# A selective scan on four engines: VectorE takes one of ScalarE's fourteen scaled copies of each round

## The reference, cut to what matters

```python
def selective_scan(u, delta, A, Bm, Cm, D):
    def step(h, inp):
        u_l, d_l, B_l, C_l = inp
        dA = jnp.exp(d_l[:, :, None] * A)
        h = h * dA + (d_l * u_l)[:, :, None] * B_l[:, None, :]
        y = jnp.einsum('bdn,bn->bd', h, C_l)
        return (h, y)
    ...
    return jnp.transpose(ys, (1, 0, 2)) + u * D
```

## Time and profile before

| | |
|---|---|
| median of 3 runs | 18361.85 us (18345.74 to 18377.84) |
| profiled execution | 18362.69 us, span 18360.9 us, mean granted clock 0.962 |
| busy share of the span | PE 88%, DVE 87%, ACT 79%, POOL 61% |
| first scan stage (`l0sf_`) | scans from 870.4 to 2913.8 us in the span |
| second scan stage (`l0sb_`) | the same work, about 3440 to 5485 us |
| granted TensorE clock in both | 1.00 |

### The profile page before, as it was taken

How to read it: one execution, slowest core, us unless ns; L and a number is a source line. 1 busy time by engine, 2 the same in 40 slices (tenths; PEclk the granted TensorE clock), 3 DMA queues, 4 the chain that set the end, 5 groups by cost and what they waited for, 6 DMA issues and landing times. The chain is left out here.

```text
span 18360.9 us, 268147 instructions
## 1 busy us (share of the span) xinstructions
PE 16077.0 (88%) x94216; PEld 11444.0 (62%) x94216; DVE 15910.4 (87%) x12063; ACT 14529.2 (79%) x23238; POOL 11254.5 (61%) x6343
## 2 busy tenths in 40 slices
PE   8799998899996788879888888888888888889798
PEld 3355554455552365455688888888888888647374
DVE  4799998799996486479899999999999999879698
ACT  7699996799992555557899999999999999745556
POOL 0099993499990475035688888888888888500201
PEclk9899999899997899989999999999999999999899
DMA  5788886788879677767777777777777777741323
GB/s 178 231 243 250 246 252 208 233 249 247 251 223 245 213 226 217 265 230 278 224 191 200 194 192 191 194 193 192 191 190 197 197 191 191 194 122 55 104 57 101
DMA packets 1043305, 3693.66 MB, mean 201 GB/s; under 512 B 162006, under 2 KB 196410, under 8 KB 1017404
## 3 DMA queue, kind: packets, MB, share of 16 engines
q1 hardware_dynamic: 815420, 3003.46, 53.8%
q0 software_dynamic: 147456, 536.94, 14.9%
q10 hardware_dynamic: 79104, 136.10, 2.4%
HBM read 2342.15 MB, written 796.94 MB: 171 GB/s over the span
## 5 line engine op out<-in xcount | busy, mean ns | idle before, releaser
L1832 DVE TENSOR_TENSOR_SCAN l1s_h<-l1s_da,l1s_pd 128x1024 f32<-128x1024 f32 x3072 | 6709.3, 2262 | 152.0 <-DMA l1s_h<-l1s_h 85.4
L1853 ACT ACTIVATE l1s_da<-l1s_dl,l1s_a 128x1024 f32<-128x1024 f32 x3072 | 3505.0, 1141 | 312.7 <-DVE l1s_h L1832 308.5
L1718 PE MATMUL l1s_pd<-l1s_bd,l1s_dut 128*128 128x128 f32 x18432 | 2847.5, 291 | 853.7 <-DVE l1s_h L1832 828.6
L1718 PEld LDWEIGHTS l1s_pd<-l1s_bd,l1s_dut 128*128 128x128 f32 x18432 | 2297.3, 191 | 1229.0 <-DVE l1s_h L1832 1092.0
L1870 ACT ACTIVATE l1s_dm<-l1s_dut,l1s_bt 128x384 f32<-128x384 f32 x5120 | 2888.2, 602 | 200.9 <-PE l1s_pd L1723 200.5
L1687 POOL TENSOR_TENSOR l1s_pb<-l1s_h,l1s_cc 128x1024 f32<-128x1024 f32 x1024 | 2423.4, 2367 | 843.7 <-DVE l1s_h L1832 802.6
L1687 POOL TENSOR_TENSOR l1s_pa<-l1s_h,l1s_cc 128x1024 f32<-128x1024 f32 x1024 | 2428.0, 2371 | 84.1 <-DMA l1s_h<-l1s_h 84.1
L1723 PE MATMUL l1s_pd<-l1s_id,l1s_dm 128*128 128x128 f32 x15360 | 2186.6, 273 | 0.1
L2702 POOL TENSOR_TENSOR l0sf_pr<-l0sf_h,l0sf_cc 128x1024 f32<-128x1024 f32 x768 | 1810.9, 2375 | 32.2 <-DVE l0sf_h L2784 27.0
L2702 POOL TENSOR_TENSOR l0sb_pr<-l0sb_h,l0sb_cc 128x1024 f32<-128x1024 f32 x768 | 1809.1, 2371 | 30.8 <-DVE l0sb_h L2784 26.8
L1723 PEld LDWEIGHTS l1s_pd<-l1s_id,l1s_dm 128*128 128x128 f32 x15360 | 1789.4, 142 | 0.6 <-ACT l1s_dm L1870 0.5
(11 more groups left out here) (323 smaller groups left out, 31362.7 us busy)
## 6 DMA issues: line engine op xcount, KB each, us to landing
l1s_cc<-crows SPq DMA_DIRECT2D x1024, 512.0 KB, 4.5
l1s_h<-l1s_h POOLq DMA_DIRECT2D x1024, 512.0 KB, 6.9
l0sf_cc<-l0crowsf SPq DMA_DIRECT2D x512, 512.0 KB, 6.3
l0sb_cc<-l0crowsb SPq DMA_DIRECT2D x512, 512.0 KB, 5.7
l0sf_cc<-l0crowsf SPq DMA_DIRECT2D x512, 256.0 KB, 8.5
l0sb_cc<-l0crowsb SPq DMA_DIRECT2D x512, 256.0 KB, 7.6
dls<-l1p_dl SPq DMA_DIRECT2D x192, 512.0 KB, 7.0
duts<-l1p_dut SPq DMA_DIRECT2D x64, 1536.0 KB, 6.6
```

The source lines that it names most:

```text
L1718: pe.matmul(pd[:, s % 2, blk * 128:blk * 128 + 128], dut[:, half, blk, j * 128:j * 128 + 128], bd[:, n, blk - SCALED, :], start=True, stop ...
L1832: dve.tensor_tensor_scan(tile(rnd, j), da[:, j, :], pd[:, s % 2, :], 0.0, ALU.mult, ALU.add)\
L1853: act.activation(da[:, j, :], dl[:, half, j, :], ACT.Exp, scale=a[:, HT * half + j, n:n + 1])\
```

## The change

VectorE makes the product of the seventh time block (index 6) for the second sequence (q = 1), in one `tensor_scalar` of 128x192 with the per-partition number B; ScalarE makes thirteen instead of fourteen. A new semaphore `multdve` tells TensorE, which now waits for four semaphores ahead of `turn_hi`.

```diff
@@ PE
                 def turn_hi(c, s):
                     pe.wait_ge(multhi, nth(c * ROUNDS + s // T))
                     pe.wait_ge(multlast, nth(c * ROUNDS + s // T))
+                    pe.wait_ge(multdve, nth(c * ROUNDS + s // T))
                     pe.wait_ge(scanhi, nth(c * STEPS + s - 1))
                     turn(s, 1).then_inc(trhi, 1)
@@ DVE
+                def multiply(c, rnd):
+                    if rnd % N == 0:
+                        loaded(dve, c, rnd // N)
+                    dve.wait_ge(trhi, nth(c * STEPS + (rnd - 1) * T - 1))
+                    out, src, b = scaled(c, rnd, LAST - 1, 1)
+                    dve.tensor_scalar(out, src, b, None, ALU.mult).then_inc(multdve, 1)
@@
                         scan_lo(c, s)
                         if not (first and s == 0):
                             scan_hi(c if s else c - 1, (s - 1) % STEPS)
+                        if j == 1 and not (final and rnd + 1 == ROUNDS):
+                            multiply(c + (rnd + 1) // ROUNDS, (rnd + 1) % ROUNDS)
                         at = s % (N * T) - 2
@@
+                multiply(0, 0)
                 chunks(dve, body)
@@ ACT
-                        for q in range(2):
+                        for q in range(1 if blk == LAST - 1 else 2):
                             out, src, b = scaled(c, rnd, blk, q)
                             ins = act.activation(out, src, ACT.Identity, scale=b)
```

More of the change, by code:

```diff
@@ L2609, in l0_scans @@
         s_u, s_y = r.dma_sem("u"), r.dma_sem("y")
-        aexp, anegd, cleared, multlo, multhi, multlast, expd, trlo, trhi, scanlo, scanhi, kept, prod, ysum, fin, passed = r.step_sems(
-            "aexp", "aneg", "cleared", "multlo", "multhi", "multlast", "expd", "trlo", "trhi", "scanlo", "scanhi", "kept", "prod", "ysum",
+        aexp, anegd, cleared, multlo, multhi, multlast, multdve, expd, trlo, trhi, scanlo, scanhi, kept, prod, ysum, fin, passed = r.step_sems(
+            "aexp", "aneg", "cleared", "multlo", "multhi", "multlast", "multdve", "expd", "trlo", "trhi", "scanlo", "scanhi", "kept", "prod", "ysum",
             "fin", "passed")
```

## The result

| | before | after |
|---|---|---|
| median | 18349.33 us (16 runs) | 18404.16 us (18395.22 to 18429.82, 16 runs) |
| ratio, 95% interval | | 1.0029, 1.0021 to 1.0037 |
| span of the profiled execution | 18360.9 us | 18400.3 us |

The account below looks back on a forecast made before the run. ACT bounds, with DVE and PE 0.6 us behind; after the change POOL does. 3 x 7.785 + 11 x 8.00 + 18.01 + 0.5 + 0.4 = 130.3 a half-chunk, +2.7, times 32 +86: 18448 us, range 18345 to 18560.

Parts of the forecast that it names:

- The bounds: Scan stages: ACT is the bound at 127.60 us a half-chunk, DVE and PE need 127.0, so at most 0.6 to gain.
- The exclusion on SBUF: DVE's new product and POOL's instructions wait for each other's whole instruction; POOL's round goes from 7.887 to 8.00 us.
- the named signs: Profile after: ACT busy 177 us less, product 0.5 to 0.8 ending 0.1 behind POOL's, POOL 8.0 a round, 130 between finishes.
- b: POOL's loss per round from waiting for DVE's new product: 0.11 us, at most 0.29.
- The room of PE: Between a low scan's end and the transposes needing it: a DVE wait of up to 0.3 us stays hidden.
- L: Time from the end of a round's first high scan to POOL's product of that step; to settle at about 0.5 us.
- `finish`: The two rounds per half-chunk holding finish, where DVE has no room: 18.01 us plus 0.5 for the two products.
- The rows of C: Rounds where POOL waits for a row of C, which a bounding POOL can't win back: 0.4 us a half-chunk.
- b = 0: Lower end: DVE's work fits into POOL's change of instruction; half-chunk 128.1 to 128.5, +16 to +29 us.
- the main case: POOL, delayed by DVE's product, sets the scan stages' pace: 130.3 us a half-chunk, +86 us; chance 0.58.
- The starved case: Rival: DVE can't get in between back-to-back POOL instructions and waits until POOL runs dry; 19060 to 19860 us, chance 0.17.

Follow-up runs that it names:

- experiment 1: Kernel before the change, with the seventh block's second-sequence product made by nobody, ScalarE making thirteen, no fourth wait; 18344.29 us, ratio 0.9995.
- experiments 2 to 4: Against the changed kernel: ScalarE makes all fourteen, VectorE's product goes to a spare tile, 1.0029; then a 128x64 transpose instead, 1.0006; last is experiment 4.
- experiment 4: Changed kernel without POOL's product of the eighth time block, which nobody makes, nor its semaphore; 18348.27 us, ratio 0.9994.
- experiments 6 and 8: Changed kernel, VectorE making the product only for rounds 3, 4, 5 of each half-chunk, 1.0009; the same with its input wait before the half-chunk's first scan, 1.0002.

## Why the prediction was right, and where its sizes were off

- **The bounds.** ACT at 127.6, the DVE and PE side at 127.0: shown by experiment 1. That nearly nothing could be gained was the step from which the rest followed.
- **The exclusion on SBUF, and who pays.** Shown by experiments 2 to 4 together: the loss stays without ScalarE's relief, and goes with either another kind of instruction or a POOL that isn't behind. The rule of the Trainium skill, "SBUF — State Buffer", section "Who interferes with whom", names `tensor_scalar` among the instructions that can enter a two-port mode and so contend with GpSimd; this case's trace agrees (0.83 beside POOL's product, 0.29 without one). Of the named signs these came: the product ending 0.1 behind POOL's, ACT's products 180 us less (177 forecast; the engine's whole busy time, of which the forecast spoke, fell by 124) and ACT waiting for DVE, POOL with almost no idle time outside `finish`. The length is at the upper end, 0.82 in the median where 0.5 to 0.8 was named, and POOL's 7.92 and the 129.0 between `finish`es are below the 8.0 and 130.
- **b was mis-sized: 0.11 forecast, 0.035 measured.** I scaled from an instruction that ended 0.28 behind POOL's. Here it ends 0.11 behind, and POOL's step across its change of instruction grows by only 0.033 (0.145 to 0.178). Nine rounds at 7.92 with five at 7.79 are 110.3, where 3 at 7.785 and 11 at 8.00 were 111.4: 1.1 too much.
- **The room of PE was mis-sized: 0.3 forecast, about 0.4 measured.** At a product of 0.60 the pitch is still 7.78 to 7.79, so a wait of 0.3 is hidden whole; at 0.83 the wait is 0.54 and costs 0.13 a round. That is why five rounds, not three, run at the old pace. It is one part of why L climbs to 0.76 instead of 0.5. The others are a slip in the forecast (a wait of L - 0.1, less 0.3 of room, costs 0.2 at L = 0.6, not 0.5) and the offset: the wait of 0.54 is L less 0.22, not less 0.1.
- **`finish` was mis-sized: +0.5 forecast, +0.75 measured.** Experiment 4 gives 0.23 of it to the second of the two rounds. The other 0.5 lies in the first one, which is entered with L settled: its product takes 0.83 where DVE has no room. From low scan to low scan, in a half-chunk of the second stage:

  | | first round with `finish` | second | rounds behind it |
  |---|---|---|---|
  | before | 9.74 | 8.26 | 7.78 |
  | experiment 4 | 9.74 | 8.50 | 7.78 |
  | the change | 10.26 | 8.50 | 7.78, then 7.92 |

- **The rows of C.** I added 0.4. The undisturbed half-chunk is 129.0 and the mean of twelve in the second stage 129.31, so it was 0.3, against 0 before in the same stage.
- Sum by the measured terms: 18.76 + 38.97 + 71.29 + 0.3 = 129.3, where 130.3 was forecast. The difference of 1.0 a half-chunk is the 31 us or so.
- **The lower end was summed too low.** For b = 0 the forecast has 128.1 to 128.5. With its own 0.5 for `finish` and 0.4 for the rows of C, 3 x 7.785 + 11 x 7.887 + 18.51 is 128.6 to 129.0, which is +33 to +46 us. So the measured +55 lies close to its case of b = 0, not halfway between that and the main case as its figures have it.
- **The starved case (0.17)** did not come in the change. Its mechanism exists, as experiments 6 and 8 show, but only one product at a time: a missed turn did not bring on the next.

## What to carry to other kernels

Work moved from an engine that is 99% busy to one that is less busy gains only down to the next bound; work that out first, `finish`-like rare steps included. Before VectorE takes an SBUF-to-SBUF `tensor_scalar`, ask how far GpSimd is behind at that moment, not how busy it is: in a loop that both share, VectorE's lead grows until its wait eats it. Where VectorE must do such a piece, a place where GpSimd waits for it costs 0.3 us, and one where GpSimd is behind costs 0.8.

## What the runs showed of the hardware that was not expected

- VectorE does get in between two GpSimd instructions that stand back to back, and the loss is small: 0.035 us of GpSimd's time for 128x192, 0.13 for 128x384. In the change this held for all 512 products.
- A second settled state exists. After a wait for a row of C (POOL idle for 1.82 us ahead of 1324.10 here; the record names nothing that ended it, and a row of C is what fits by the code), POOL is nearly one product further behind, and DVE gets in between the two products of a pair instead; it then waits less. DVE and POOL of the changed kernel:

```profile
1384.57 0.48 DVE L2793 TENSOR_SCALAR l0sf_dm<-l0sf_dut,l0sf_bt 128x192 f32<-128x192 f32 x1
...
1392.50 0.48 DVE L2793 TENSOR_SCALAR l0sf_dm<-l0sf_dut,l0sf_bt 128x192 f32<-128x192 f32 x1
```

```profile
1390.48 4.72 POOL L2702 TENSOR_TENSOR l0sf_pr<-l0sf_h,l0sf_cc 128x1024 f32<-128x1024 f32 x2
```

  The pair's first product ends half-way, near 1392.84, and DVE's ends at 1392.98. The round is 7.93 all the same: POOL sets it, whichever boundary is used.
- In the two kernels in which DVE makes the product for three rounds of sixteen (experiments 6 and 8), 12 of the 64 first products of a half-chunk waited through three boundaries (3.7 to 3.8 us).
- A float32 block transpose of VectorE, 128x64 from SBUF to SBUF, never waited for GpSimd: 0.211 to 0.245 us in 512 cases.
